# Merging norm, weight preparation and table building of each graph-attention layer into one stage, and the softmax inverse as exp(-ln)

## The reference, cut to what matters

```
x = relu-normed x                          # no gain, no shift
for i in range(2):
    xl = (x @ Wl[i] + bl[i]).reshape(n, H, C)
    xr = (x @ Wr[i] + br[i]).reshape(n, H, C)
    s = leaky_relu(xl[src] + xr[dst], 0.2)
    e = einsum('ehc,hc->eh', s, att[i])
    ex = exp(e - segment_max(e, dst)[dst])
    alpha = ex / segment_sum(ex, dst)[dst]
    out = segment_sum(alpha[:, :, None] * xl[src], dst)
    x = relu(layer_norm(out.mean(axis=1) + bias[i] + x, ln_g[i], ln_b[i]))
```

## Time and profile before

| | |
|---|---|
| median of three runs | 3101.64 us |
| the profiled execution: its own time, its span | 3132.41 us, 3130.6 us |
| mean granted TensorE clock | 0.922 of full |
| busy: PE, DVE, ACT, POOL | 75%, 71%, 40%, 26% of the span |
| layer 0, first bn_stats to the start of gat_scores | 564.26 to 655.82 us |
| layer 1, the same | 1675.09 to 1775.40 us |
| softmax inverse to the end of ACT's last copy | 1373.64 to 1398.18 us, and once more in layer 1 |

### The profile page before, as it was taken

How to read it: one execution, slowest core, us unless ns; L and a number is a source line. 1 busy time by engine, 2 the same in 40 slices (tenths; PEclk the granted TensorE clock), 3 DMA queues, 4 the chain that set the end, 5 groups by cost and what they waited for, 6 DMA issues and landing times. The chain is left out here.

```text
span 3130.6 us, 52451 instructions
## 1 busy us (share of the span) xinstructions
PE 2350.9 (75%) x12514; PEld 1551.1 (50%) x12628; DVE 2237.7 (71%) x10715; ACT 1249.0 (40%) x2770; POOL 826.8 (26%) x883
## 2 busy tenths in 40 slices
PE   3775796578888788737885788887788378857999
PEld 1443684234444444416664344444444156645777
DVE  5667666868888888884558688888888944466654
ACT  1776893332222222213354523222222123356654
POOL 0000100036666566500000265666665100000000
PEclk8999898789999999969997899999999689978999
DMA  0000600269999999617543489999988065436221
GB/s 26 1 2 3 282 7 15 91 202 277 276 278 275 271 274 278 193 29 177 159 111 83 159 266 273 277 275 282 275 274 270 4 155 160 137 86 251 80 64 38
DMA packets 418141, 519.14 MB, mean 166 GB/s; under 512 B 31943, under 2 KB 353090, under 8 KB 416450
## 3 DMA queue, kind: packets, MB, share of 16 engines
q0 software_dynamic: 66560, 274.39, 28.0%
q1 hardware_dynamic: 349996, 239.60, 26.4%
q10 hardware_dynamic: 1302, 1.80, 0.2%
HBM read 414.74 MB, written 100.93 MB: 165 GB/s over the span
## 5 line engine op out<-in xcount | busy, mean ns | idle before, releaser
L963 POOL DMA_INDIRECT rows<-row_table,idx x832 | 789.2, 949 | 813.5 <-POOLq L140 307.8
L1014 PE MATMUL z_ps<-xr,hot_ta 128*128 x2400 | 673.6, 388 | 246.1 <-DVE rows L1065 196.6
L1025 PE MATMUL z_ps<-rows,ident 128*128 128x256 f32 x1664 | 576.5, 428 | 10.4 <-issue 10.4
L1014 PEld LDWEIGHTS z_ps<-xr,hot_ta 128*128 128x128 bf16 x2496 | 245.0, 98 | 538.9 <-issue 407.9
L1065 DVE SCALAR_TENSOR_TENSOR rows<-rows,att_all 128x128 f32<-128x128 f32 x1664 | 429.5, 294 | 77.7 <-remote 37.1
L1090 DVE TENSOR_TENSOR rows<-z_ps,rows 128x256 f32<-128x256 f32 x832 | 347.5, 418 | 132.7 <-PE z_ps L1025 89.4
L1065 DVE SCALAR_TENSOR_TENSOR rows<-z_ps,att_all 128x128 f32<-128x128 f32 x1664 | 410.0, 280 | 25.5 <-issue 25.3
L1405 PE MATMUL acc_m<-xr,hot_m 128*128 x1984 | 341.2, 293 | 76.3 <-issue 53.2
L1405 PEld LDWEIGHTS acc_m<-xr,hot_m 128*128 128x128 f32 x1984 | 281.9, 194 | 142.0 <-issue 136.6
L1036 ACT ACTIVATE spread_a<-spread_a,below 128x512 bf16<-128x512 bf16 x208 | 149.9, 721 | 447.8 <-PE z_ps L1025 379.9
L1025 PEld LDWEIGHTS z_ps<-rows,ident 128*128 128x128 f32 x1664 | 257.3, 195 | 112.0 <-issue 18.3
(11 more groups left out here) (460 smaller groups left out, 3673.6 us busy)
## 6 DMA issues: line engine op xcount, KB each, us to landing
xr<-kept_rows SPq DMA_DIRECT2D x124, 512.0 KB
kept_rows<-rows SPq DMA_DIRECT2D x416, 128.0 KB
spread_a<-rel_rows SPq DMA_DIRECT2D x208, 128.0 KB
counts_line<-counts SPq DMA_DIRECT2D x1, 19550.0 KB
counts<-counts_line SPq DMA_DIRECT2D x6, 3200.0 KB, 10.0
rows<-row_table,idx POOLq DMA_INDIRECT x832
row_table<-xl_ring SPq DMA_DIRECT2D x50, 258.0 KB
rows<-row_table SPq DMA_DIRECT2D x32, 320.0 KB, 7.0
```

The costliest lines, as they stand in the source:

```text
L963: nc.gpsimd.indirect_dma_start(out=rows[:, u, :], out_offset=None, in_=table, in_offset=bass.IndirectOffsetOnAxis(ap=c.idx[:, n:n + 1], ax ...
L1014: nc.tensor.matmul(ps[:, n % Z, :], hot, tile[:, m, 0:HC], start=m == 0, stop=False, skip_group_check=True)
L1025: nc.tensor.matmul(ps[:, n % Z, HALF_C:HC], c.ident[:, :], rows[:, n % ROWS, HALF_C:HC], start=False, stop=True, skip_group_check=True).th ...
```

## The change

1. `norm_relu` ahead of each attention layer and `gat_weights` are gone; their work stands in `gat_tables`, in the same phase as the tables. The eight loads are issued at that phase's start. DVE takes all statistics, then waits for the eight loads, makes lin_w and b_sum, and only then the inverse of the square root. The tiles are normalised one by one inside the tile loop: on ACT alone in layer 0, and in layer 1 by two DVE instructions a tile (four and three tiles of them ahead of the loop) and one relu on ACT.
2. b_out is computed on DVE behind the tile loop.
3. h is stored in five DMAs of five tiles, each behind a tile of xl, the last behind the last tile.
4. In the softmax the totals are added head by head, and the inverse is exp(-ln(total)) on ACT: four ln, then four exp, with an idle ln on one column ahead of them.

The last `norm_relu`, behind layer 1, stays as it was.

```diff
+                nc.scalar.activation(idle[:, :], c.ident[:, 0:1], ACT.Sqrt)
+                act.wait_ge(s["varied"], 1)
+                nc.scalar.activation(std[:, :], std[:, :], ACT.Sqrt).then_inc(s["std"], 1)
+                def normed(t):
+                    if gain is None:
+                        if t == 0:
+                            act.wait_ge(s["inverse"], 2)
+                        nc.scalar.activation(h[:, t, :], x[:, t, :], ACT.Relu, bias=norm_bias[:, t:t + 1],
+                                             scale=rstd[:, t:t + 1]).then_inc(s["normed"], 1)
+                        return
+                    act.wait_ge(s["shifted"], t + 1)
+                    nc.scalar.activation(h[:, t, :], h[:, t, :], ACT.Relu).then_inc(s["normed"], 1)
...
+                for t in range(AHEAD - 1):
+                    normed(t)
                 take_turned(0)
                 for t in range(NODE_TILES):
+                    if t + AHEAD - 1 < NODE_TILES:
+                        normed(t + AHEAD - 1)
...
             def _(dve):
+                for t in range(NODE_TILES):
+                    nc.vector.bn_stats(stats[:, t, :], x[:, t, :]).then_inc(s["stats"], 1)
...
+                dve.wait_ge(s["loads"], 16 * LOADS)
+                for head in range(H):
+                    last = nc.vector.scalar_tensor_tensor(
...
+                link(nc.vector.tensor_tensor(out=g.b_sum[:, :], in0=g.b_sum[:, :], in1=g.bl_all[:, :], op=ALU.add))
+                dve.wait_ge(s["std"], 1)
+                nc.vector.reciprocal(rstd[:, :], std[:, :]).then_inc(s["inverse"], 1)
...
+                for t in range(AHEAD + 1):
+                    scaled(t)
+                for t in range(AHEAD):
+                    shifted(t)
                 link(nc.vector.memset(bias_parts[:, :], 0.0))
...
                 for t in range(NODE_TILES):
+                    scaled(t + AHEAD + 1)
+                    shifted(t + AHEAD)
                     dve.wait_ge(s["left"], t + 1)
...
-                sp.dma_start(table.rearrange("(t p) c -> p t c", p=P)[:, :, XLW:ROW], h).then_inc(s["h_stored"], 16)
+                loads(sp, s["loads"])
...
+                    if t % STORE == STORE - 1:
+                        low = t + 1 - STORE
+                        sp.wait_ge(s["normed"], t + 1)
+                        sp.dma_start(table.rearrange("(t p) c -> p t c", p=P)[:, low:t + 1, XLW:ROW],
+                                     h[:, low:t + 1, :]).then_inc(s["h_stored"], 16)
...
+                nc.scalar.activation(idle[:, :], c.ones[0:SB, 0:1], ACT.Ln)
+                for h in range(H):
+                    act.wait_ge(s["total"], h + 1)
+                    total = split(run)[:, :, h, :]
+                    nc.scalar.activation(total, total, ACT.Ln).then_inc(s["log"], 1)
+                for h in range(H):
+                    act.wait_ge(s["log"], h + 1)
+                    total = split(run)[:, :, h, :]
+                    nc.scalar.activation(total, total, ACT.Exp, scale=-1.0).then_inc(s["inverse"], 1)
```

More of the change, by code:

```diff
@@ L723, in weight_loads, with gat_tables @@
     return issue
[L726 to L746, removed]
+def gat_tables(nc, c, g, x, h, table, loads, gain=None, shift=None):
     RIGHTS = 4
+    LOADS = 8
     with ExitStack() as ctx:
@@ L775, in lin @@
             return small[:, t % 2, P:P + H]
-        with phase(nc, const=0, turned=0, h_t=0, left=0, right=0, xl=0, lin=0, z=0, first=0, rest=0, second=0, third=0,
+        STORE = 5
+        AHEAD = 3
+        with phase(nc, loads=0, stats=0, var=0, varied=0, std=0, inverse=0, scaled=0, shifted=0, normed=0, lin_w=0,
+                   const=0, turned=0, h_t=0, left=0, right=0, xl=0, lin=0, z=0, first=0, rest=0, second=0, third=0,
                    scored=0, parts=0, stored=RING, h_stored=0) as (block, s):
@@ new lines, in _ @@
+                dve.wait_ge(s["loads"], 16 * LOADS)
+                for head in range(H):
+                    last = nc.vector.scalar_tensor_tensor(
+                        out=prod[:, :], in0=g.w[0][:, head * C:(head + 1) * C], scalar=SLOPE,
+                        in1=g.att[:, head * C:(head + 1) * C], op0=ALU.mult, op1=ALU.mult,
+                        accum_out=g.w[0][:, HC + head:HC + head + 1])
+                    if head + 1 < H:
+                        link(last)
+                last.then_inc(s["lin_w"], 1)
@@ new lines, in scaled, with shifted @@
+                def scaled(t):
+                    if gain is not None and t < NODE_TILES:
+                        nc.vector.scalar_tensor_tensor(out=h[:, t, :], in0=x[:, t, :], scalar=mean_var[:, t, 0:1],
+                                                       in1=gain, op0=ALU.subtract, op1=ALU.mult)\
+                          .then_inc(s["scaled"], 1)
+                def shifted(t):
+                    if gain is not None and t < NODE_TILES:
+                        dve.wait_ge(s["scaled"], t + 1)
+                        nc.vector.scalar_tensor_tensor(out=h[:, t, :], in0=h[:, t, :], scalar=rstd[:, t:t + 1],
+                                                       in1=shift, op0=ALU.mult, op1=ALU.add).then_inc(s["shifted"], 1)
@@ L891, in _ @@
                     third_part(t)
+                for head in range(H):
+                    link(nc.vector.scalar_tensor_tensor(out=g.b_out[:, :], in0=g.bl_all[:, head * C:(head + 1) * C],
+                                                        scalar=1.0 / H, in1=g.b_out[:, :], op0=ALU.mult, op1=ALU.add))
                 dve.wait_ge(s["lin"], NODE_TILES)
@@ L1144, in gat_softmax @@
         with phase(nc, masked=0, turned=0, es_rows=0, breaks=0, keeps=0, scanned=0, ends=0, slots=0, over=0, carried=0,
-                   fixed=0, less=0, ex=0, vec=0, alpha=0, back=0, moves=0) as (block, s):
+                   fixed=0, less=0, ex=0, total=0, log=0, inverse=0, vec=0, alpha=0, back=0, moves=0) as (block, s):
             @block.gpsimd
```

43 lines of the change are left out of this document (34 added, 9 removed).

## The result

The changed kernel takes 3087.3 us (median of 6 runs, 3083.45 to 3088.99); the kernel before, on the same chip, 3102.01 (6 runs). The ratio is 0.9945 [0.9933, 0.9958], and the forecast was 3086.5.

A forecast was written before the change was run, and what follows sets the result against it. Fronts serial on DVE, DVE and PE nearly tied in the tile loop (2.27 of 2.48 us); -7.6 - 15.2 + 6.3 + 2.5 - 1.1 = -15.1 us from 3101.64 gives 3086.5 us, range 3081.5 to 3093.5.

The forecast's parts named there:

- When the loads land: Start of both table stages: loads land at 572.15 and 1682.20, costing about a microsecond of waiting, no more.
- the front of layer 0: Before layer 0's first z: it starts at 581.27 instead of 588.83, 7.6 us gained; up to 0.5 may show.
- Rival 5: Layer 0's front: waits keep the first z where it was, 7.6 us less gained, 3094.1 us; chance 0.04.
- Front of layer 1: Before layer 1's first z: it starts at 1693.18 instead of 1708.42, 15.2 us gained.
- Loop of layer 0: Layer 0's tile loop: DVE unchanged, ACT's normalised tile fits its idle time; cost 0, or 2.4 us if tiles run late.
- Loop of layer 1: Layer 1's tile loop: two more DVE instructions a tile make DVE the bound at 2.80 us; 6.3 us lost.
- Rival 1: Layer 1's loop: two dependent passes cost full durations, 14.6 us instead of 6.3, 3094.8 us in all; chance 0.12.
- rival 4: Layer 1's loop: gaps drop TensorE to 1.2 GHz, 3.78 us a tile, 3108.1 us in all; chance 0.04.
- Tail: Behind the tile loops: b_out costs 1.27 us in each layer, 2.5 in all; last store of h 0, up to 1.
- Softmax: Softmax: PE's first head starts 0.55 us earlier a layer, 1.1 in all; 13.4 us of reciprocals removed give nothing more.
- Rival 2: Softmax: the switch back to exp costs more than its 1.28 us, 3089.1 us in all; chance 0.12.
- Rival 3: Softmax: TensorE's clock may rise earlier, 2 x 1.7 us more gained, 3083.1 us, or the reverse; chance 0.08.

The follow-up runs named there:

- passes_ahead: The changed kernel with all 50 passes of the layer-1 norm on DVE ahead of the bias chain, none in the loop; ratio 0.9971 to the kernel before.
- best: The changed kernel with norm scalars ahead of the loads' wait, layer-1 norm (tiles 3 to 24) and b_out on GpSimd, zero matmuls on PE; ratio 0.9923 to before.
- merge_only: The changed kernel with the old softmax (one add, four reciprocals); ratio 0.9933 to the kernel before.
- soft_only: The kernel before with only the new softmax (adds by head, ln and exp); ratio 0.9992 to the kernel before.
- busy_pe2: The changed kernel with more zero matmuls on PE: 43 ahead of the transposes, 18 ahead of the bias matmul, 53 ahead of softmax's first head; ratio 0.9931 to before.
- after_again: The changed kernel run once more, unaltered, in a later set; median 3108.27 us, ratio 0.9946 to the kernel before.
- head0_recip: The changed kernel with softmax head 0 inverted by DVE's reciprocal behind all four adds, heads 1 to 3 by ln and exp; ratio 0.9939 to before.
- busy_pe: The changed kernel with zero matmuls on waiting PE: 26 ahead of the tables' transposes, 10 ahead of the bias chain, 36 ahead of softmax's first head; ratio 0.9945 to before.
- best2: The kernel best with zero matmuls resized: 36, 8 and 18 in the tables, 53 ahead of softmax's first head; 3076.84 us, ratio 0.9911 to before.
- best3: The kernel best2 without the zero matmuls in the tables, only the 53 ahead of softmax's first head; ratio 0.9916 to before.
- pool_norm: The changed kernel with the layer-1 norm passes of tiles 3 to 24 on GpSimd instead of DVE; median 3108.24 us, ratio 0.9939 to before.

## Why the prediction was right

- **When the loads land, and the front of layer 0.** DVE was to wait about a microsecond (1.13 us seen) and the first z was to come 17.0 us behind the first statistics; it came at 16.72. The up to 0.5 us that I kept for ACT's late tile 0 did not show. Rival 5 falls.
- **Front of layer 1.** Forecast 18.1, seen 19.44, and 18.27, 18.68 and 19.00 where the same front ran again. The loads are what varies: DVE waited 2.02, 0.67, 1.08 and 1.58 us for them, and without that wait all four fronts take 17.4 to 17.6 us. The landing at 1682.20 that the sum used left a wait of 0.3 us only. Gained: 13.9 us, not 15.2.
- **Loop of layer 0.** 2.48 us as before; cost 0, as forecast. The stage gained 1.5 us more, nearly all of it because the second z followed the first by 2.38 and not 3.78: the clock.
- **Loop of layer 1.** The mechanism is as forecast, DVE the bound and hardly ever idle, PE's weight loads waiting for it, clock 1.00. The size was a little off: the 2.27 us of DVE's work were 2.20, because z overlaps the copy ahead of it when it need not wait, and so the pace is 2.72, not 2.80. From first to last z it is 64.27 us instead of 60.77, 3.5 us rather than 6.3. Of the 2.8 us between, 1.3 are the pace (4.5 us from tile 1 on, where I had 5.8), and 1.5 the first tile, where I charged 0.5 and it gave 1.0 back: there the clock was up sooner (2.73 us from the first z to the second at a granted clock of 1.00, where before took 3.77 at 0.63). passes_ahead, with the passes taken out, goes back to 2.483, so they are the cause of the pace. Rival 1 (14.6 us) and rival 4 fall: 2.72 us a tile leaves TensorE at its high level. The Trainium skill's "A second HAM failure mode: psum-queue depth-cycling" (page "TensorE: Matmul & The Clock Gate") speaks of short idles of PE between groups of matmuls; PE's row shows next to none here (47.81 of 48 us busy, clock 1.00), so no run here puts it to the test.
- **Tail.** 1.27 us forecast for b_out in each layer. The stretch from last z to scores grew by 1.16 and 1.17 us, and it shrank by 1.07 in best, where b_out is off DVE. The store of h costs nothing: SP waits 1.6 us for it and 1.2 for the xl store, and then 2.8 us for the others. After's waits of SP, 1733 to 1742 us:

```profile
SPq L137 <- PEq L137: 2.8, 1, 2.8
SPq L980 <- DMA row_table<-h: 1.6, 1, 1.6
SPq L980 <- DMA row_table<-xl_ring: 1.2, 1, 1.2
```

- **Softmax.** 0.55 us forecast for PE's start, 0.57 seen in after and 0.58 between merge_only's and soft_only's rows. Four reciprocals off DVE bring no 13 us. Rival 2 falls on the row itself, where nothing stands between the last ln (ends 1354.64), the load (1354.66) and exp (1355.95). The drain of the page "ScalarE: Activation LUTs", section "What ACT_TABLE_LOAD costs" in the Trainium skill, isn't seen in this place; by it PE would have started 0.8 us later than before, and it starts 0.57 earlier.
- **Rival 3, the clock.** It happened in part, in both directions. With ln and exp, the same 32 matmuls behind a rest take 16.6 or 15.5 us in one execution or another of the same code, and 13.54 where PE is kept busy (busy_pe2). after's profile had two short ones, after_again's one. With the reciprocal, PE's start 6.55 to 6.63 us behind the add, all six groups on record took 16.4 to 16.9 us (before, merge_only, head0_recip, two layers each). With ln and exp, at 5.98, and no zeros ahead, seven of twelve took 15.2 to 15.6 and five 16.6 to 16.9. So the earlier start may often bring an earlier clock too, 1.1 us more than I counted; twelve groups don't prove it. With zeros ahead the high clock can be had on purpose.
- **Sum.** In after's profile the stages give 8.2 and 9.2 us and the two softmaxes 2.0 and 1.7, 21 in all, where the forecast had 15.1 and the runs show 14.7 by medians and 17 by the ratio. after_again's profile has 7.9 to 8.0, 9.7, 0.9 and 1.7, 20. Without what the clock gave in the first tiles (2.4 us) and in the groups of 32 (2.5), after's sum is 16.1: layer 1's front gained 1.3 us less than forecast, its loop cost 1.8 less, and the rest is within 0.3 each. So the forecast's terms hold, two of them with errors of 1.3 and 1.8 us that point in opposite directions. That the time itself, 3087.3, lies within 0.8 us of 3086.5 is in part luck, since these errors nearly cancel, and the clock's part came on top in the profile where I had counted it at 0. Why four to six of the 21 us don't reach the total is open. Part of it can be that two single executions are compared: 1.7 us of layer 1's gain are gone when soft_only's profile stands for before.

## What to carry to other kernels

Passes over all tiles in front of a loop can go into the loop even when that loop then becomes bound by their engine: what counts is what they cost there (4.5 us) against what they held up in front (11.5). A cheaper function on a long operation is worth only the start of the first piece where the next engine is booked from there on; look at when that engine starts, not at the busy time that goes. Before a burst of matmuls behind a long rest, ask at what clock they begin: here the burst was 1.9 to 3.4 us too long for that alone, more than the 0.57 us that the softmax edit gave PE's start.

## What the runs showed of the hardware

- TensorE's clock came down behind a rest of 3.9 us (busy_pe: 1.00 in 569 to 572, 0.70, then 0.50), and did not behind 0.50 to 1.05 us (busy_pe2, best2, best3: all six groups of 32 matmuls take 13.54 us). When it rises again varies between executions: with the same front of layer 1, the second z came 2.73, 2.72, 3.85 and 4.44 us behind the first (after, after_again, head0_recip, merge_only). The granted clock in that stretch was 1.00 in after and 0.57 in merge_only; with the zeros of best2 it was 1.00 (2.25 us), without them in best3 0.55 (4.25 us).
- DVE's 128x128 instruction with both tensors in SBUF lasts 352 ns beside GpSimd's work and 284 ns behind it (pool_norm), while the 128x512 instructions that read PSUM keep their 680 to 692 ns. GpSimd's 128x128 subtract and multiply takes 907 ns on average. Moving two passes there (0.52 us a tile of DVE) gave back 0.12 of the 0.24 us that the pace had lost.
- DVE's pass with a scalar from memory lasts 0.35 us, but the next instruction starts 0.26 us behind its start, in a row of 25 (6.65 us) and in the table loop alike. For a sum of work the distance of the starts counts, not the durations. Idle time read from the rows (0.21 us) is a little less than the room there is (0.28 us), since an instruction that need not wait starts before the one ahead of it ends.
- A reciprocal of 104x512 in 32 bits takes 3.34 us on DVE, where the product of the same shape takes 0.69.
